# Two position attentions of a transformer stack, their batches written out instead of looped

## The reference, cut to what matters

```
scores = einsum('bqhd,bkhd->bhqk', q, k) + einsum('bqr,bkr->bqk', q_rope, k_rope)[:, None]
scores = where(causal, -inf, scores / sqrt(40));  w = softmax(scores)
attn   = einsum('bhqk,bkhd->bqhd', w, v);  x = x + attn @ W_o
```

## Time and profile before

| | us |
|---|---|
| median of 3 runs | 3052.63 |
| lowest, highest | 3051.08, 3052.76 |
| the profiled execution's own time | 3054.7 |
| its span, first to last instruction | 3052.9 |
| mean granted TensorE clock over the span | 0.861 of 2.4 GHz |
| layer 0's attention, first score product to last `osb` copy | 224.1 to 806.5 |
| layer 1's attention, last `osb` copy ends | 2156.9 |

### The profile page before, as it was taken

The page is one execution under the profiler, slowest core; times in us unless marked ns, Lnnn a source line. Parts: engine busy times, 40 slices in busy tenths (PEclk is TensorE's granted clock), DMA queues, the critical chain, the costliest instruction groups (busy, mean ns, idle before and its releaser), DMA issues. The chain is left out here.

```text
span 3052.9 us, 47721 instructions
## 1 busy us (share of the span) xinstructions
PE 2288.3 (75%) x13512; PEld 1237.1 (41%) x13512; DVE 1721.6 (56%) x5414; ACT 1303.1 (43%) x2495; POOL 487.9 (16%) x524
## 2 busy tenths in 40 slices
PE   3549999999685048777999999999676381977282
PEld 1214444444353026522444444444454270654262
DVE  3647676777235976275666656665366124666323
ACT  2406565666355545363444444544132141342140
POOL 1400000000003000051000000000044471043554
PEclk9859999999787559887999999999788595988596
DMA  4272545452120002153122221221300242000154
GB/s 131 78 142 54 99 84 102 83 102 41 39 72 3 1 8 78 22 152 85 44 60 54 52 55 44 61 55 33 122 17 29 67 142 71 1 4 20 47 142 124
DMA packets 177914, 199.90 MB, mean 65 GB/s; under 512 B 36384, under 2 KB 117920, under 8 KB 177568
## 3 DMA queue, kind: packets, MB, share of 16 engines
q1 hardware_dynamic: 160000, 173.72, 22.8%
q0 software_dynamic: 9216, 19.02, 1.9%
q10 hardware_dynamic: 8448, 4.20, 0.5%
HBM read 127.09 MB, written 69.76 MB: 64 GB/s over the span
## 5 line engine op out<-in xcount | busy, mean ns | idle before, releaser
L928 ACT ACTIVATE at_probs<-at_score 128x512 f32<-128x512 f32 (+3 forms) x1536 | 718.3, 491 | 693.6 <-PE at_score L838 591.7
L806 PE MATMUL at_mx<-at_K,at_Q 96*128 96x512 bf16 (+7 forms) x1536 | 515.3, 341 | 78.0 <-DMA at_K<-k 38.8
L950 DVE CUSTOM_DVE_ANT_0 at_masked<-at_mx,g_maskw 128x512 bf16<-128x512 f32 (+3 forms) x1024 | 477.4, 488 | 158.9 <-PE at_mx L806 154.2
L833 PE MATMUL at_score<-at_Q,at_K 96*128 96x512 bf16 (+7 forms) x1536 | 506.2, 330 | 32.3 <-DMA at_Q<-m 16.8
L835 PE MATMUL at_score<-at_Q,at_K 98*128 98x512 bf16 (+7 forms) x1536 | 502.6, 330 | 0.0
L947 DVE TENSOR_REDUCE at_mpart<-at_mx 128x1 f32<-128x512 f32 x512 | 352.2, 688 | 168.8 <-PE at_mx L806 167.8
L855 PE MATMUL at_outp<-at_probs,at_vop 128*32 128x512 f32 (+6 forms) x3072 | 444.3, 497 | 0.0
L806 PEld LDWEIGHTS at_mx<-at_K,at_Q 120*128 120x128 bf16 (+1 forms) x1536 | 149.5, 99 | 284.2 <-issue 64.9
L833 PEld LDWEIGHTS at_score<-at_Q,at_K 120*128 120x128 bf16 (+1 forms) x1536 | 150.4, 98 | 277.4 <-issue 121.3
L1033 POOL MEMSET n_spread<- 16x128 f32 (+1 forms) x2 | 0.7, 354 | 1429.1 <-POOLq L644 1429.1
L838 PE MATMUL at_score<-g_maskkq,g_identb 128*128 128x128 bf16 x1024 | 225.2, 220 | 0.0
(11 more groups left out here) (467 smaller groups left out, 3463.6 us busy)
## 6 DMA issues: line engine op xcount, KB each, us to landing
at_Q<-q SPq DMA_DIRECT2D x192, 128.0 KB, 3.0
at_Q<-qr SPq DMA_DIRECT2D x72, 256.0 KB, 6.7
at_K<-kr SPq DMA_DIRECT2D x72, 256.0 KB, 7.8
q<-p_pieces SPq DMA_DIRECT2D x40, 384.0 KB, 3.3
at_K<-k SPq DMA_DIRECT2D x168, 64.0 KB, 2.3
buf<-g_zeros SPq DMA_DIRECT2D x32, 325.0 KB, 5.2
o<-at_osb SPq DMA_DIRECT2D x64, 128.0 KB
n_oc<-o SPq DMA_DIRECT2D x8, 1024.0 KB, 4.9
```

The lines of the kernel that those rows point to most:

```text
L806: pe.matmul(mx[:, u % MB, 0:hi - lo], Q0[0:R, g % 4, j, qt * P:(qt + 1) * P], K0[0:R, g % 4, j % KG, lo:hi], start=True, stop=True).then_i ...
L833: pe.matmul(bank, K0[0:R0, g % 4, j % KG, kb * P:(kb + 1) * P], Q0[0:R0, g % 4, j, lo:hi], start=True, stop=False)
L928: act.activation(probs[:, kb % 2, j, lo:hi], score[:, h % SB, lo - half * CH:CH], ACT.Exp, scale=cf.scale).then_inc(s_exp, 1)
L950: dve.tensor_tensor_reduce(masked[:, u % MB, 0:w], mx[:, u % MB, 0:w], k.maskw[:, CH - w:CH], 1.0, NEG, ALU.add, ALU.max, mpart[:, part, j ...
```

## The change

In `attention`, the loop over batches 0 to 2 becomes a Python loop over all four, so every step is written out in each engine's stream, with constants for the semaphore values and addresses. The helpers that served the loop's registers (`tok`, the `isinstance` tests) go. Order of work, tiles, buffers, semaphores and transfers stay.

```diff
-        tok = {}
-
         def first_token(b):
-            return b * T if isinstance(b, int) else tok[b is tok["b"]]
+            return b * T

         def nxt(b, g):
-            return (b, g + 1) if g + 1 < GN else (tok["b1"] if tok.get("b") is b else b + 1, 0)
+            return (b, g + 1) if g + 1 < GN else (b + 1, 0)

         def ahead(b, g, m):

-            if isinstance(b, int) and b == NB - 1 and g + m >= GN:
+            if b == NB - 1 and g + m >= GN:
                 return None
...
         def over_batches(eng, step):

-            with eng.Fori(0, NB - 1) as b:
-                tok.clear()
-                if eng is nc.sync:
-                    tok.update({"b": b, "b1": b + 1, True: eng.snap(b * T), False: eng.snap(b * T + T)})
+            for b in range(NB):
                 for g in range(GN):
                     step(b, g)
-            tok.clear()
-            for g in range(GN):
-                step(NB - 1, g)
```

## The result

The changed kernel takes 3025.03 us (median of 4 executions, 3021.39 to 3030.68) against 3051.86 us before (4 executions beside it, 3050.68 to 3052.76): a ratio of 0.9914, 95% interval 0.9898 to 0.9930. The forecast was 3025.3. The profiled execution of the changed kernel was the slowest of its four, 3030.68 us, with a span of 3027.8 us.

What follows compares the result with a forecast made beforehand. PE's stream was taken to bound both attentions. Jumps 24.0 plus registers 3.3 us, other parts zero, made 27.3 us, taking the profiled 3054.7 to 3027.4, and the median to 3025.3; range 3020 to 3034.

Steps and rivals of the forecast that it cites:

- ruler: Distance between DVE's once-a-step copies as step length: written-out steps take 36.06 us in layer 0, 22.945 in layer 1.
- Part 1: Four jumps back, two in each attention, go: 24.0 us won, 15.0 of PE gaps and about 9 of lost clock.
- Part 2: ACT's 1.28 us table load at each of the four jumps goes, covered by PE's own gap: zero.
- Part 3: Loop registers behind the waits' compare values go from both attentions' steps: 3.3 us won, bounds 0 and 4.
- Part 4: SP's address registers go and batch loads are wanted 5 to 7 us sooner: zero, upper bound 8 us lost.
- Part 5: Two further copies of each body on four engines: zero, plus or minus 3 us for clock changes in other stages.
- rival C: Slower: PE runs out of straight code inside batches, 6.0 us a stop; 3097 with one in 12 layer 0 steps; 2%.
- The bounds as listed (3, 5, 3 and 1): Range allowances in us: registers may give 0, table loads or operand waits, other stages, and the median itself.
- A: The gap belongs to a batch's start, not the jump, so only the registers' 3.3 us are won: 3049.3; 4%.
- B: Half the gain: shorter gaps with the clock still falling, or short operand waits instead; 13.6 us won, 3039; 8%.

Runs made afterwards that it cites:

- hinted_loop: Kernel before with its loop kept, each engine's branch back given a hint at the head of the body naming its target; ratio 0.9971 to before.
- the loop sizes: Changed kernel plus a leading stage of PE-only loops of different body sizes: no stop at 400 to 1600 instructions, mostly 2.3 to 2.8 us a jump from 1720.
- pause_long: Changed kernel with PE held at the starts of batches 1 and 2 until GpSimd has filled a tile of 4800 columns; ratio 0.9998 to before.
- act_looped: Kernel before with every engine's stream written out except ACT's, which alone keeps the loop; ratio 0.9941 to before.
- early_exp: Changed kernel with one exponential of one element ahead of ACT's first wait in each attention; ratio 0.9910 to before.
- pe_looped: Kernel before with DVE, ACT and SP written out and only PE keeping the loop; 3046.90 us, ratio 0.9989 to before.
- one_pass_loops: Kernel before with batches 0 to 2 as three loops of one pass each on all four engines, no branch back taken; 3026.82 us against 3049.03.

## Why the prediction was right, point by point

- **Bound and ruler.** Batch 3 of the kernel before was already the changed kernel, and its step, 36.06 and 22.945 us, is the step of all batches now. That is why the sum came out within 1 us where the trace measures it: 26.97 us in the two stretches, for which the prediction's parts give 24.0 + 2.6 + 0.5 = 27.1. That the median after, 3025.03, met the forecast of 3025.3 within 0.3 us is luck: the interval of the ratio alone is 10 us wide, and the second time the kernel took 3020.76, 30.4 us less than before.
- **Part 1, the jumps: 24.0 us.** Measured 24.0: the passages are at the ruler's length. That "issue" was the wait for code was argued there and is shown now, by hinted_loop and the loop sizes. The split into 15.0 of gap and 9 of clock is borne out by pause_long (16.1 and 9.4). The ground given for it, a body above 2048 instructions, was the right kind of reason with a wrong number. The row read for it was another engine's: q14 is not PE's queue, which is q8, and that moved 3 packets in the same 29.8 us against 1 in the step.
- **Part 2, table loads: zero.** Right for the four at the jumps, which PE's own stop hid; in act_looped, without that stop, ACT's stop with its load of 1.28 us costs 1.2 to 3.5 us a passage. Missed: the loop had its first load ahead of the wait, and written out it stands behind it. PE did not wait for it (early_exp), so the zero holds.
- **Part 3, registers: 3.3 us.** In layer 0 the three times 0.87 came, 12.69 - 10.02 = 2.67. In layer 1 it was 14.28 - 14.01 = 0.27 in place of 0.50, because one step, 1443.34 to 1466.57, takes 23.23 us, and one 23.02, in each kernel whose DVE is written out. What stops there is not settled. They go with DVE's loop; the prediction named no engine. The 0.2 us for the first step of each loop can't be seen: from the first score product to the first copy layer 0 took 0.57 and layer 1 0.79 us longer than before, at a lower clock.
- **Part 4, SP and the loads: zero.** Right; PE waits for no operand at any passage.
- **Part 5, longer code: zero, plus or minus 3 for other stages.** The longer code adds no stop but the 0.3 us in one step and 0.1 in another, if these are its doing, so rival C didn't occur. The 3 was too small: over the traces here, what lies between and outside the copies of the attentions takes from 1779.2 us (hinted_loop) to 1792.9 (pe_looped), while the earlier three runs of before had suggested 2.
- **The range.** The bounds as listed (3, 5, 3 and 1) add up to 3021 to 3037, and not to 3020 to 3034; the 8 us of part 4 were left out of it.
- **Rivals.** A is excluded by one_pass_loops. B, a half of the gain, did not occur, but it is what one gets when only PE is written out (10.7 us of the 24.0 stay at the passages).

## What to carry to other kernels

Where a loop peels its last pass, the trace holds a free forecast of what writing it out will do: measure the peeled steps against the looped ones with an instruction that comes once a step. A loop whose body is longer than the code an engine keeps (only PE's limit was measured here) pays at each jump for the fetch and, on TensorE, often for the clock after it. Writing it out removes that; a shorter body should too, which was not tried in the attentions. Do it on all engines that work in step, since the next engine's stop takes the place of the one removed. Before a difference of 1 or 2 us is given to an edit, compare the granted clock of the two stretches.

## What the runs showed of the hardware that was not expected

- PE keeps less code than a body of 1720 instructions (products and weight loads) needs and enough for one of 1600; above, the jump back costs 2.3 to 2.8 us in a bare loop, 3.5 to 3.9 in these attentions.
- A hint for the branch back takes PE's stop from 3.53 to 0.66 us, but at the loop's end, where the jump isn't taken, DVE stopped for 4.99 us.
- A stop of 1.80 us can already be followed by the lower clock, or not: 3.06 against 1.48 us; both stops of 1.90 us were, at 3.58. Stops of 2.50 and 2.57 us cost 2.31 and 4.05. Each of the four stops of near 4 us cost 1.3 to 3.2 us beyond its own length.
- The stops of engines that work in step don't add: all four engines' jumps cost 24.0 us, PE's alone 24.4, and those of the other three, without PE's, 10.7 (DVE's alone 12.2, ACT's alone 9.4; in each of these two the clock fell at two of the four passages).
- Over the twelve traces of these kernels, layer 1's attention took 25.03 to 26.65 us from its first score product to its first copy, and the granted clock of the second 4 us, 1.00 to 0.66, goes with it.
